# Last stage: residual rows and the experts' second sum through accumulating DMAs, the gates' silu one chunk later

## The chip, the cores and the metric

The kernel runs on one core of a Trainium2 chip. The metric is the device time of one execution in microseconds (us): 5662.19 us, the median of 3 runs (5662.12 to 5663.08). The engines are called by short names: PE is TensorE (PEld its weight loads), DVE is VectorE, ACT is ScalarE, POOL is GpSimd, SP is SyncE, which here only starts transfers.

## What is computed

Four sequences of 2048 tokens with 256 channels go through two layers. The first is a Mamba scan gated by two layers of local attention. The second, to which the change belongs, ends like this in the reference (cut):

```python
xn = _layernorm(x)
s = _L1_attn_ref(xn, ...)        # linear attention over gelu(q)+0.21, gelu(k)+0.21, then
                                 # (res - mu) / sqrt(var + 1e-12) * gamma + beta, res = out + xn
g = _silu(_L1_ffn_ref(xn, ...))  # 64 experts, the best 6 per token, 128 slots each, plus a shared expert
return x + s * g
```

`x` on the last line is the residual: the result of the first layer. The argument of the silu is a sum of three things: the shared expert and the contributions of the routed experts.

## The kernel before, in words

The program runs in blocks, one after the other. In each block every engine has its own written-out list of instructions in order, and semaphores tie them together; no planner is at work. The blocks are set-up, the scan (`mamba`), `layers` (local attention, its gated parts, and `route`), `experts` and `final`.

`route` goes through the 8192 tokens in 16 chunks of 512 (a tile of 128 partitions x 4 x 256). `store_sum` writes the mixed rows x to the DRAM tensor `x1_d`, `store_norm` writes xn and the scores to `xe_d`; the shared expert's output goes to `y_d`, and `odd_d` is cleared.

`experts` goes through the 64 experts. POOL gathers 128 rows per expert with an indirect DMA (L2424) and adds the weighted results back by an indirect accumulating DMA (L2439), even experts into `y_d` (`moe_out`), odd ones into `odd_d` (`moe_odd`). Meanwhile SP loads the first tiles that the last stage needs (`FirstTiles`, `last_stage_chunk`), for chunks 0 and 1 also the residual rows `x1`.

`final` is the last stage, 16 chunks again. Names in the profile are those of the tiles: `ym` is fym, `yo` is fyo, `s1` is fs, `o` is fo, `rot` is frot, `qT` is fqT, `tab` is ftab, `rs` is frs, `x1` is fx. Per chunk c:

- SP (`load_rows`, `load_sums`): loads ym and yo from `y_d` and `odd_d`, xn and x1, three buffers each; a buffer is free when the residual add of the chunk three before it is done (`s_fin`). Then SP waits for `s_fin` of chunk c and stores s1 to the output. ACT's queue loads the transposed xn (`xT`). Each is 512 KB.
- PE: `queries(c+1)` (L2545), then `attend(c)`: L2566 for the normaliser and L2576 for the output. L2566 waits until DVE has read the one buffer p_z of the chunk before (L2676).
- ACT: `queries(c+1)` (L2616, gelu), then `gates(c+1)` (L2622, silu of ym), which waits for POOL's `join`. In the first four chunks `keep_tables` (L2607), which copies the turned rope tables out of PSUM, stands ahead of them in the list.
- DVE: `rotate(c+1)` (L2645), `normaliser(c)` (L2676 zz, L2681 rz, L2714 variance of chunk c-1, L2688 o = p_o * rz, L2694 o += xn), `finish(c-1)` (L2724, L2730, L2735: subtract mean, gamma, rstd, beta, gate), `moments(c)` (L2702, L2708). In three iterations `key_means` is added.
- POOL: `power(c)` (L2760, rstd from the variance, wanted by L2730), `join(c+2)` (L2775, ym += yo; it waits for `s_re`, that is for L2694 of chunk c+1), `residual(c)` (L2767, s1 += x1, after L2735 of chunk c).

Of the kernel before, what the change touches and what calls it, by code (L numbers as in the profile page):

```python
# [8 lines left out]
F32 = mybir.dt.float32  # L9
# [62 lines left out]
def program(nc, A, out, book):  # L72
    xs = nc.dram_tensor("stream", [NS * SLOTS * P, D], F32).ap()
    ssm_out = nc.dram_tensor("ssm_out", [CH + T, D], F32).ap()
    x1_d = nc.dram_tensor("x1", [T, D], F32).ap()
    xe_d = nc.dram_tensor("rows_and_scores", [T, ROW], F32).ap()
# [12 lines left out]
    with ExitStack() as top:  # L89
        def const(name, shape, dt=F32):  # L90
            return top.enter_context(nc.sbuf_tensor(name, shape, dt))

        ident = const("ident", [P, P])
        identb = const("identb", [P, P], BF16)
        mhalf = const("mhalf", [P, 2 * H])
        zrow = const("zrow", [P, D])
        take, put = const("take", [P, NE], I32), const("put", [P, NE], I32)

        with nc.cleanup_on_exit(), ExitStack() as ctx:
            setup(nc, ctx, ident, identb, mhalf, zrow)  # L100
        with nc.cleanup_on_exit(), ExitStack() as ctx:
            mamba(nc, ctx, A, rows, x_in, ssm_out, qk_d, ident, mhalf, zrow)

        cs = const("rope", [P, CPB, CT, 2, D])
        with nc.cleanup_on_exit(), ExitStack() as ctx:
            layers(nc, ctx, A, rows, x_in, ssm_out, x1_d, xe_d, xt_d, y_d, odd_d, kv_d, qk_d, take, put, ident, identb, mhalf,
                   zrow, cs)
        with nc.cleanup_on_exit(), ExitStack() as both:
            first = FirstTiles(nc, both)
            with nc.cleanup_on_exit(), ExitStack() as ctx:  # L110
                experts(nc, ctx, A, x1_d, xe_d, xt_d, y_d, odd_d, kv_d, take, put, ident, first)
            with nc.cleanup_on_exit(), ExitStack() as ctx:
                final(nc, ctx, A, x1_d, xe_d, xt_d, y_d, odd_d, kv_d, out_rows, ident, mhalf, first, cs)

# [1530 lines left out]

def layers(nc, ctx, A, rows, x_in, ssm_out, x1_d, xe_d, xt_d, y_d, odd_d, kv_d, qk_d, take, put, ident, identb, mhalf, zrow, cs):


    bottom = nc.sbuf_base
    with ExitStack() as own:  # L1650
# [6 lines left out]
        g1 = gated(nc, ctx, A, rows, 1, ident, mhalf, gt, at, a1)  # L1657
    rt = route(nc, ctx, A, rows, x_in, ssm_out, x1_d, xe_d, xt_d, y_d, odd_d, kv_d, take, put, ident, mhalf, zrow, cs,
               gt.top - bottom, high - gt.top, g1)
# [51 lines left out]

def route(nc, ctx, A, rows, x_in, ssm_out, x1_d, xe_d, xt_d, y_d, odd_d, kv_d, take, put, ident, mhalf, zrow, cs, first_gap, second_gap, before):

# [79 lines left out]
    def sync(sp):  # L1793
# [651 lines left out]

def final(nc, ctx, A, x1_d, xe_d, xt_d, y_d, odd_d, kv_d, out_rows, ident, mhalf, first, cs):
# [4 lines left out]
    xn, x1 = (t + [sb(f"{n}{k}", [P, CT, D]) for k in range(2, NB)] for t, n in ((first.xn, "fxn"), (first.x1, "fx1")))
    ym, yo = ([sb(f"{n}{k}", [P, CT, D]) for k in range(NB)] for n in ("fym", "fyo"))
    xT, kv, w_q, brow, blk, gam, bet = first.xT, first.kv, first.w_q, first.brow, first.blk, first.gam, first.bet
# [34 lines left out]
    with nc.Block() as block:  # L2488
        @block.sync
        def _(sp):  # L2490
            def load_sums(f):
                k = f % NB
                if f >= NB:
                    sp.wait_ge(s_fin, f - NB + 1)
                sp.dma_start(ym[k][:], tiles(y_d[f * CH + 1:(f + 1) * CH + 1, :])).then_inc(s_ym[k], 16)
                sp.dma_start(yo[k][:], tiles(odd_d[f * CH + 1:(f + 1) * CH + 1, :])).then_inc(s_yo[k], 16)

            def load_rows(f):
                k, rowsf = f % NB, slice(f * CH, (f + 1) * CH)
# [99 lines left out]
        def _(act):  # L2599
# [28 lines left out]
            queries(0)  # L2628
            gates(0)
            for c in range(NC):  # L2630
                if c + 1 < CPB:
                    keep_tables(c + 1)
                if c + 1 < NC:
                    queries(c + 1)
                    gates(c + 1)

        @block.vector
        def _(dve):
# [77 lines left out]
            def finish(c):  # L2716
                k = c % 2
                if c > 1:
                    dve.wait_ge(s_out[k], 16 * (c // 2))
                if c == 0:  # L2720
                    dve.wait_ge(s_gb, 32)
                dve.wait_ge(s_mv, c + 1)
                for j in range(CT):
                    ins = dve.scalar_tensor_tensor(out=s1[k][:, j], in0=o[k][:, j], scalar=mv[k][:, j, 0:1],  # L2724
                                                   in1=gam[:], op0=ALU.subtract, op1=ALU.mult)
# [9 lines left out]
                dve.tensor_tensor(out=s1[k][:], in0=s1[k][:], in1=ym[c % NB][:], op=ALU.mult).then_inc(s_gate, 1)  # L2735

# [20 lines left out]
        def _(pool):  # L2757
# [79 lines left out]
```

## Time and profile before

| | |
|---|---|
| median of 3 runs | 5662.19 us |
| the profiled execution, its own time | 5660.84 us |
| its span in the profile | 5659.1 us |
| busy over the span | PE 87%, PEld 52%, DVE 75%, ACT 52%, POOL 52% |
| last stage (from the first instruction of `final` at 5393.8 us) | 265 us of the span |
| one chunk in the middle of the last stage | 14.79 us |
| HBM read and written | 425.05 MB and 180.37 MB |

The profile is one execution on the chip. Times of rows are in us from the start of the span. "Busy" of an engine is the time in which it executes instructions; a row of the timeline or of the groups names the line, the engine, the operation, the tile written and the tiles read, and in brackets how long the engine sat idle before it and which instruction released it. The share of an engine over the whole span says little about a stage: the last stage is 5% of the span and has its own limit.

### The profile page before, as it was taken

How to read it: one execution, taken by the hardware profiler on the slowest of the kernel's cores; microseconds unless marked ns; L12 is line 12 of the kernel's file. 1: busy time of each engine (PE TensorE's matmuls, PEld its weight loads, DVE VectorE, ACT ScalarE, POOL GpSimd, SP SyncE). 2: the span in 40 equal slices, each digit the busy share in tenths (PEclk: the TensorE clock that was granted, in tenths of full speed). 3: DMA queues.
4: the chain of work that ended last, by engine and by line, in shares of the span. 5: the costliest groups of instructions: out<-in, count | busy, mean ns of one | idle time of the engine just before them, and what ended most of it. 6: DMA issues, size and time to landing. Idle time of an engine off the chain costs nothing. (4 is left out here: it accounts for less than half of the span.)

```text
span 5659.1 us, 79616 instructions
## 1 busy us (share of the span) xinstructions
PE 4948.7 (87%) x26068; PEld 2924.1 (52%) x26068; DVE 4225.2 (75%) x8753; ACT 2969.3 (52%) x6267; POOL 2968.3 (52%) x1603
## 2 busy tenths in 40 slices
PE   7788778777876599999999999999999999998876
PEld 2223223222322377777555566666665556666765
DVE  3999999999999799999433377777763338994279
ACT  4776776776776477777211255555541114452232
POOL 4999889988998556556111244444421010004733
PEclk9898999988987699999999999999999999999987
DMA  5665566556555222323112111111111134445645
GB/s 132 146 156 143 131 150 152 147 131 148 149 146 123 69 90 83 91 91 108 44 49 73 44 35 35 38 35 37 53 42 56 56 104 157 154 143 143 174 159 180
DMA packets 501470, 593.79 MB, mean 105 GB/s; under 512 B 59702, under 2 KB 380996, under 8 KB 496964
## 3 DMA queue, kind: packets, MB, share of 16 engines
q1 hardware_dynamic: 486756, 579.36, 37.3%
q10 hardware_dynamic: 2016, 7.34, 0.4%
q0 software_dynamic: 12288, 2.00, 0.3%
q8 instruction: 211, 3.46, 0.3%
q14 instruction: 199, 1.63, 0.1%
HBM read 425.05 MB, written 180.37 MB: 107 GB/s over the span
## 5 line engine op out<-in xcount | busy, mean ns | idle before, releaser
L654 POOL TENSOR_TENSOR db<-durep,brep 128x2048 f32<-128x2048 f32 x256 | 1161.8, 4538 | 187.9 <-DVE p_h L561 176.9
L513 ACT ACTIVATE p_h<-dlrep,am 128x512 f32<-128x512 f32 x1024 | 704.4, 691 | 195.7 <-DVE hh L572 170.7
L561 DVE TENSOR_TENSOR_SCAN p_h<-p_h,hlast,db 128x512 f32<-128x512 f32 x576 | 716.4, 1273 | 0.0
L349 PE MATMUL p_acc<-hh,fold 128*32 128x512 f32 x2048 | 315.5, 692 | 341.9 <-DVE hh L572 340.7
L1267 POOL TENSOR_TENSOR rot_cos<-rot_cos,rot_sin 128x1024 f32<-128x1024 f32 x128 | 302.5, 2363 | 535.4 <-DVE rot_sin L1188 535.4
L1263 POOL TENSOR_TENSOR rn<-n,mhalf 128x16 f32<-128x16 f32 x128 | 375.2, 2931 | 265.7 <-DVE n L1198 265.6
L572 DVE TENSOR_TENSOR hh<-p_h,crep 128x512 f32<-128x512 f32 x768 | 513.0, 668 | 0.0
L1630 POOL TENSOR_TENSOR grstd<-grstd,mhalf 128x4 f32<-128x4 f32 x32 | 32.6, 1019 | 730.7 <-DVE grstd L1547 730.5
L945 PE MATMUL p_s<-qkT 64*128 64x128 f32 x4096 | 300.0, 286 | 75.7 <-DVE nb L1153 74.6
L1532 ACT ACTIVATE gg<-p_s,b 128x512 f32<-128x512 f32 x160 | 110.0, 687 | 449.0 <-PE p_o L1475 266.2
L1056 ACT ACTIVATE probB<-probB,nb 128x256 f32<-128x256 f32 x512 | 254.3, 499 | 164.7 <-DVE nb L1153 164.7
L642 POOL TENSOR_TENSOR hh<-hs,crep 128x512 f32<-128x512 f32 x256 | 328.2, 1282 | 12.8 <-DVE hs L561 12.8
L349 PEld LDWEIGHTS p_acc<-hh,fold 128*32 128x32 f32 x2048 | 42.4, 114 | 559.9 <-DVE hh L572 535.4
L945 PEld LDWEIGHTS p_s<-qkT 64*128 64x128 f32 x4096 | 250.6, 189 | 129.0 <-DVE nb L1153 105.6
L1475 PE MATMUL p_s<-ghT,w 128*128 128x512 f32 x640 | 302.9, 596 | 5.2 <-DVE ghid L1584 3.6
L1496 PE MATMUL p_t<-w,ghid 128*128 128x256 f32 x1280 | 284.8, 382 | 0.0
L976 PE MATMUL p_o<-probT,v 128*64 128x128 f32 x4096 | 280.2, 279 | 3.0 <-DVE probT L1171 3.0
L561 DVE TENSOR_TENSOR_SCAN hs<-p_h,hlast,db 128x512 f32<-128x512 f32 x192 | 244.0, 1271 | 49.2 <-ACT p_h L513 46.8
L1067 ACT ACTIVATE probT<-p_t 128x512 f32<-128x512 f32 x256 | 152.1, 594 | 232.5 <-PE p_t L962 232.5
L1171 DVE COPY probT<-p_t 128x512 f32<-128x512 f32 x256 | 175.9, 687 | 127.9 <-PE p_t L962 127.8
L502 ACT ACTIVATE hlast<-p_h 128x1 f32<-128x1 f32 x576 | 95.4, 166 | 329.8 <-DVE hh L572 328.7
L227 PE MATMUL p_f<-mxT,w_in 128*128 128x512 f32 x512 | 260.1, 655 | 8.1 <-ACT mxT L390 5.5
(285 smaller groups left out, 11939.4 us busy)
## 6 DMA issues: line engine op xcount, KB each, us to landing
dlrep<-delta_rows SPq DMA_DIRECT2D x256, 256.0 KB
durep<-drive_rows SPq DMA_DIRECT2D x256, 256.0 KB
ew<-in_L_ffn_w SPq DMA_DIRECT2D x192, 176.0 KB
first_queries_keys<-qs SPq DMA_DIRECT2D x128, 256.0 KB, 2.1
qk<-first_queries_keys SPq DMA_DIRECT2D x64, 512.0 KB, 3.8
brep<-bc_rows SPq DMA_DIRECT2D x64, 256.0 KB
crep<-bc_rows SPq DMA_DIRECT2D x64, 256.0 KB
delta_rows<-dl SPq DMA_DIRECT2D x64, 256.0 KB
```

The source lines that it names most:

```text
L349: ins = pe.matmul(p_acc[32 * j:32 * j + 32, :], fold[:], hh[s % 2][:, j], start=False, stop=(g == NG - 1), skip_group_check=True)
L513: act.activation(p_h[:, (i % BANKS) * CH:(i % BANKS + 1) * CH], dlrep[use % 2][:, j], ACT.Exp, scale=am[:, q, j, g:g + 1]).then_inc(s_ex, 1)
L561: dve.tensor_tensor_scan(out=state, data0=bank, data1=db[s % 2][:, j], initial=0.0 if first else hlast[:, i % TILES:i % TILES + 1], op0=AL ...
L572: dve.tensor_tensor(out=hh[s % 2][:, j], in0=p_h[:, (i % BANKS) * CH:(i % BANKS + 1) * CH], in1=crep[c % 2][:, s % NG], op=ALU.mult).then_ ...
L642: pool.tensor_tensor(out=hh[s % 2][:, 0], in0=hs[s % 2][:], in1=crep[c % 2][:, s % NG], op=ALU.mult).then_inc(s_hp, 1)
L654: pool.tensor_tensor(out=db[s % 2][:], in0=durep[use % 2][:], in1=brep[c % 2][:, g:g + 1, :].to_broadcast([P, 4, CH]), op=ALU.mult).then_i ...
L945: ins = pe.matmul(p_s[:, at:at + P], here[g * DK:(g + 1) * DK, c:c + P], there[g * DK:(g + 1) * DK, INNER + c:INNER + c + P], start=True, ...
L976: ins = pe.matmul(p_o[g * DK:(g + 1) * DK, (h // 2) * P:(h // 2 + 1) * P], vv[u][:, h * DK:(h + 1) * DK], probT[:, j, w, :], start=(w == 0 ...
L1263: pool.tensor_tensor(out=rn[f % 2][:], in0=n2[f % 2][:], in1=mhalf[:], op=ALU.pow).then_inc(s_rn, 1)
L1267: pool.tensor_tensor(out=rc[:], in0=rc[:], in1=rsn[:], op=ALU.add).then_inc(s_rot, 1)
L1475: ins = pe.matmul(dst[:], w1[:, f, o + j * P:o + (j + 1) * P], hT[:, f, :], start=(f == 0), stop=(f == DH - 1))
L1496: ins = pe.matmul(p_y[:, j0 * D:(j0 + 1) * D], hid[:, j, j0 * P:(j0 + 1) * P], w2[:, j, :], start=False, stop=(j == FB - 1), skip_group_ch ...
```

## The change

Six edits, all in or for the last stage:

1. The residual rows are stored by `route` straight into the output tensor instead of `x1_d`, which is gone. The loads of x1 (two in `experts`, fourteen in `final`) are gone with their tiles and semaphores.
2. POOL's `residual(c)` no longer adds: it issues a DMA that adds s1 onto the output rows in DRAM (`accum_op`). SP's store of the output and its wait are gone.
3. POOL's `join(c)` no longer adds: after ym has landed it issues a DMA that adds the rows of `odd_d` onto ym in SBUF. The loads of yo and their tiles are gone, and so is the wait for `s_re`.
4. ACT's `gates(c)` waits for that DMA and stands in iteration c, behind `queries(c+1)`, instead of one iteration earlier; `gates(0)` no longer stands ahead of the loop.
5. SP's loads wait for `s_gate` (L2735 done) instead of `s_fin`.
6. s1 has three buffers instead of two; `finish(c)` waits for the accumulating DMA of chunk c-3.

```diff
 # route
-            sp.dma_start(tiles(x1_d[f * CH:(f + 1) * CH, :]), x[f % 2][:]).then_inc(s_sx1[f % 2], 16)
+            sp.dma_start(tiles(out_rows[f * CH:(f + 1) * CH, :]), x[f % 2][:]).then_inc(s_sx1[f % 2], 16)
 # experts, last_stage_chunk
-                sp.dma_start(first.x1[f][:], tiles(x1_d[rowsf, :])).then_inc(first.s_x1[f], 16)
 # final, sync
                 if f >= NB:
-                    sp.wait_ge(s_fin, f - NB + 1)
+                    sp.wait_ge(s_gate, f - NB + 1)
                 sp.dma_start(ym[k][:], tiles(y_d[f * CH + 1:(f + 1) * CH + 1, :])).then_inc(s_ym[k], 16)
-                sp.dma_start(yo[k][:], tiles(odd_d[f * CH + 1:(f + 1) * CH + 1, :])).then_inc(s_yo[k], 16)
...
                 sp.dma_start(xn[k][:], tiles(xe_d[rowsf, 0:D])).then_inc(s_xn[k], 16)
-                sp.dma_start(x1[k][:], tiles(x1_d[rowsf, :])).then_inc(s_x1[k], 16)
...
-                sp.wait_ge(s_fin, c + 1)
-                sp.dma_start(tiles(out_rows[c * CH:(c + 1) * CH, :]), s1[c % 2][:]).then_inc(s_out[c % 2], 16)
 # final, scalar
             def gates(c):
-                act.wait_ge(s_ya, c + 1)
+                act.wait_ge(s_yo[c % NB], 16 * (c // NB + 1))
                 act.activation(ym[c % NB][:], ym[c % NB][:], ACT.Silu).then_inc(s_sy, 1)
...
             queries(0)
-            gates(0)
             for c in range(NC):
                 if c + 1 < CPB:
                     keep_tables(c + 1)
                 if c + 1 < NC:
                     queries(c + 1)
-                    gates(c + 1)
+                gates(c)
 # final, vector, finish(c): s1[k] becomes s1[n], n = c % NB
-                if c > 1:
-                    dve.wait_ge(s_out[k], 16 * (c // 2))
+                if c >= NB:
+                    dve.wait_ge(s_out[n], 16 * (c // NB))
 # final, gpsimd
             def residual(c):
-                pool.wait_ge(s_x1[c % NB], 16 * (c // NB + 1))
                 pool.wait_ge(s_gate, c + 1)
-                pool.tensor_tensor(out=s1[c % 2][:], in0=s1[c % 2][:], in1=x1[c % NB][:], op=ALU.add).then_inc(s_fin, 1)
+                pool.dma_start(tiles(out_rows[c * CH:(c + 1) * CH, :]), s1[c % NB][:],
+                               accum_op=ALU.add).then_inc(s_out[c % NB], 16)
 
             def join(c):
                 k = c % NB
-                if c > 1:
-                    pool.wait_ge(s_re, c)
                 pool.wait_ge(s_ym[k], 16 * (c // NB + 1))
-                pool.wait_ge(s_yo[k], 16 * (c // NB + 1))
-                pool.tensor_tensor(out=ym[k][:], in0=ym[k][:], in1=yo[k][:], op=ALU.add).then_inc(s_ya, 1)
+                pool.dma_start(ym[k][:], tiles(odd_d[c * CH + 1:(c + 1) * CH + 1, :]),
+                               accum_op=ALU.add).then_inc(s_yo[k], 16)
...
+            for k in range(NB):
+                pool.wait_ge(s_out[k], 16 * len(range(k, NC, NB)))
```

## Rows read from the trace of the kernel before

**Rows 1.** Busy time by stretch: one chunk (14.79 us), and the stretch with the lowest clock

```profile
core 0: us, PE busy (x) PEld busy (x) DVE busy (x) ACT busy (x) POOL busy (x), PEclk, DMA share, GB/s
5522.94:5537.73 14.79, 12.27 (x65) 9.99 (x65) 14.41 (x24) 4.89 (x5) 5.89 (x3) 0.84 0.65 206
5565.00:5580.00 15.00, 13.38 (x56) 11.15 (x56) 14.58 (x30) 4.89 (x5) 5.89 (x3) 0.66 0.63 205
```

**Rows 2.** Timeline of PE in the last stage: what its normaliser waits for

```profile
5521.01 3.55 PE L2566 MATMUL fp_z<-fkm,fqT 128*128 128x8 f32 x16 [2.50 <-DVE zz L2676]
```

**Rows 3.** Timeline of DVE, part of one chunk (start, us, engine, line, tiles)

```profile
5521.61 1.23 DVE L2688 TENSOR_TENSOR fo<-fp_o,rz 128x1024 f32<-128x1024 f32 x1
5522.94 1.23 DVE L2694 TENSOR_TENSOR fo<-fo,fxn 128x1024 f32<-128x1024 f32 x1
5524.08 3.77 DVE L2724 SCALAR_TENSOR_TENSOR fs<-fo,fmv,gam 128x256 f32<-128x256 f32 x4
...
5532.47 3.06 DVE L2645 SCALAR_TENSOR_TENSOR frot<-fqT,ftab 128x1024 f32<-128x1024 f32 x2
```

**Rows 4.** Timeline of POOL in the same chunk

```profile
5521.62 1.02 POOL L2760 TENSOR_TENSOR frs<-frs,mhalf 128x4 f32<-128x4 f32 x1 [3.11 <-DVE frs L2714]
5524.25 2.53 POOL L2775 TENSOR_TENSOR fym<-fym,fyo 128x1024 f32<-128x1024 f32 x1 [1.60 <-DVE fo L2694]
5530.97 2.34 POOL L2767 TENSOR_TENSOR fs<-fs,fx 128x1024 f32<-128x1024 f32 x1 [4.19 <-DVE fs L2735]
```

**Rows 5.** Timeline of DVE where POOL is idle beside it

```profile
5410.83 2.36 DVE L2645 SCALAR_TENSOR_TENSOR frot<-fqT,ftab 128x1024 f32<-128x1024 f32 x2 [3.05 <-ACT fqT L2616]
...
5640.47 1.67 DVE L2724 SCALAR_TENSOR_TENSOR fs<-fo,fmv,gam 128x256 f32<-128x256 f32 x4
```

**Rows 6.** The chain that ended last, in order of time, at the stage's start

```profile
5428.71 2.52 POOL fym L2775
5431.26 1.06 ACT fym L2622
...
5433.92 6.22 PE fp_q L2545 x8
```

**Rows 7.** Timeline of PE, ACT and DVE at the stage's start

```profile
5403.74 1.06 ACT L2622 ACTIVATE fym<-fym 128x1024 f32<-128x1024 f32 x1
...
5406.40 3.67 PE L2545 MATMUL fp_q<-fxT,w_q 128*128 128x512 f32 x8 [2.39 <-ACT ftab L2607]
...
5440.98 2.36 DVE L2645 SCALAR_TENSOR_TENSOR frot<-fqT,ftab 128x1024 f32<-128x1024 f32 x2 [3.98 <-ACT fqT L2616]
...
5446.29 1.23 DVE L2688 TENSOR_TENSOR fo<-fp_o,rz 128x1024 f32<-128x1024 f32 x1 [1.10 <-PE fp_o L2576]
```

**Rows 8.** Groups of POOL's instructions in `experts`: gathers and accumulating scatters of 128 rows

```profile
L2424 POOL DMA_INDIRECT ex<-rows_and_scores,take x64 | 67.3, 1051 | 20.2 <-issue 17.1 <-POOL ex L2428 0.9 <-DMA moe_out<-eyb,put 0.9
L2439 POOL DMA_INDIRECT moe_out<-eyb,put x32 | 50.8, 1589 | 29.3 <-DVE eyb L2415 16.5 <-issue 8.3 <-DMA moe_out<-eyb,put 4.5
```

**Rows 9.** DMA queues (packets, MB, share of 16 engines), stretch 5385.5 to 5387.3

```profile
q0 software_dynamic: 117, 0.11, 56.4%
```

**Rows 10.** The same, stretch 5653 to 5660: the last store of the output

```profile
q1 hardware_dynamic: 528, 0.52, 21.1%
```

**Rows 11.** The chain again: a load of yo from its issue to its landing

```profile
5623.54 5.60 DMA fyo<-moe_odd
```

**Rows 12.** Timeline of DVE and POOL at the end of the stage

```profile
5638.00 1.22 DVE L2688 TENSOR_TENSOR fo<-fp_o,rz 128x1024 f32<-128x1024 f32 x1
...
5649.22 1.67 DVE L2730 SCALAR_TENSOR_TENSOR fs<-fs,frs,bet 128x256 f32<-128x256 f32 x4
...
5645.24 2.34 POOL L2767 TENSOR_TENSOR fs<-fs,fx 128x1024 f32<-128x1024 f32 x1 [6.22 <-DVE fs L2735]
5647.69 1.19 POOL L2760 TENSOR_TENSOR frs<-frs,mhalf 128x4 f32<-128x4 f32 x1
5652.30 2.34 POOL L2767 TENSOR_TENSOR fs<-fs,fx 128x1024 f32<-128x1024 f32 x1 [3.42 <-DVE fs L2735]
```

More of the change, by code:

```diff
@@ L105, in program @@
         with nc.cleanup_on_exit(), ExitStack() as ctx:
-            layers(nc, ctx, A, rows, x_in, ssm_out, x1_d, xe_d, xt_d, y_d, odd_d, kv_d, qk_d, take, put, ident, identb, mhalf,
+            layers(nc, ctx, A, rows, x_in, ssm_out, out_rows, xe_d, xt_d, y_d, odd_d, kv_d, qk_d, take, put, ident, identb, mhalf,
                    zrow, cs)
@@ L110, in program @@
             with nc.cleanup_on_exit(), ExitStack() as ctx:
-                experts(nc, ctx, A, x1_d, xe_d, xt_d, y_d, odd_d, kv_d, take, put, ident, first)
+                experts(nc, ctx, A, xe_d, xt_d, y_d, odd_d, kv_d, take, put, ident, first)
             with nc.cleanup_on_exit(), ExitStack() as ctx:
-                final(nc, ctx, A, x1_d, xe_d, xt_d, y_d, odd_d, kv_d, out_rows, ident, mhalf, first, cs)
+                final(nc, ctx, A, xe_d, xt_d, y_d, odd_d, kv_d, out_rows, ident, mhalf, first, cs)
 def allocators(nc, ctx, tag=""):
@@ L1643, in gated, with layers @@
     return Programs(tensor, scalar, vector, gpsimd, sync, s_out, s_y=s_y)
-def layers(nc, ctx, A, rows, x_in, ssm_out, x1_d, xe_d, xt_d, y_d, odd_d, kv_d, qk_d, take, put, ident, identb, mhalf, zrow, cs):
+def layers(nc, ctx, A, rows, x_in, ssm_out, out_rows, xe_d, xt_d, y_d, odd_d, kv_d, qk_d, take, put, ident, identb, mhalf, zrow, cs):
     bottom = nc.sbuf_base
@@ L1657, in layers @@
         g1 = gated(nc, ctx, A, rows, 1, ident, mhalf, gt, at, a1)
-    rt = route(nc, ctx, A, rows, x_in, ssm_out, x1_d, xe_d, xt_d, y_d, odd_d, kv_d, take, put, ident, mhalf, zrow, cs,
+    rt = route(nc, ctx, A, rows, x_in, ssm_out, out_rows, xe_d, xt_d, y_d, odd_d, kv_d, take, put, ident, mhalf, zrow, cs,
                gt.top - bottom, high - gt.top, g1)
@@ L1709, in __init__, with route @@
         self.tensor, self.scalar, self.vector, self.gpsimd, self.sync = tensor, scalar, vector, gpsimd, sync
-def route(nc, ctx, A, rows, x_in, ssm_out, x1_d, xe_d, xt_d, y_d, odd_d, kv_d, take, put, ident, mhalf, zrow, cs, first_gap, second_gap, before):
+def route(nc, ctx, A, rows, x_in, ssm_out, out_rows, xe_d, xt_d, y_d, odd_d, kv_d, take, put, ident, mhalf, zrow, cs, first_gap, second_gap, before):
     sb, ps, sem = allocators(nc, ctx)
@@ L2297, in __init__ @@
         self.kv = [sb(f"fkv{k}", [P, 2 * D]) for k in range(2)]
-        self.xn, self.x1 = ([sb(f"{n}{k}", [P, CT, D]) for k in range(2)] for n in ("fxn", "fx1"))
+        self.xn = [sb(f"fxn{k}", [P, CT, D]) for k in range(2)]
         self.w_q, self.brow, self.blk = sb("w_q", [P, DH, D]), sb("fbrow", [P, D]), sb("fblk", [P, P])
@@ L2301, in __init__, with experts @@
         self.s_w, self.s_blk, self.s_gb = sem("f_weights"), sem("f_blk"), sem("f_gamma_beta")
-        self.s_xT, self.s_kv, self.s_xn, self.s_x1 = (
-            [sem(f"f_{n}{k}") for k in range(2)] for n in ("xT", "kv", "xn", "x1"))
-def experts(nc, ctx, A, x1_d, xe_d, xt_d, y_d, odd_d, kv_d, take, put, ident, first):
+        self.s_xT, self.s_kv, self.s_xn = (
+            [sem(f"f_{n}{k}") for k in range(2)] for n in ("xT", "kv", "xn"))
+def experts(nc, ctx, A, xe_d, xt_d, y_d, odd_d, kv_d, take, put, ident, first):
     sb, ps, sem = allocators(nc, ctx)
@@ L2443, in _, with final @@
                 pool.wait_ge(s_add[e % U], 16 * (NE // U))
[L2446 removed]
+def final(nc, ctx, A, xe_d, xt_d, y_d, odd_d, kv_d, out_rows, ident, mhalf, first, cs):
     sb, ps, sem = allocators(nc, ctx)
     NB, HH = 3, HA // DH
[L2451 to L2452 removed]
+    xn = first.xn + [sb(f"fxn{k}", [P, CT, D]) for k in range(2, NB)]
+    ym = [sb(f"fym{k}", [P, CT, D]) for k in range(NB)]
     xT, kv, w_q, brow, blk, gam, bet = first.xT, first.kv, first.w_q, first.brow, first.blk, first.gam, first.bet
@@ L2461, in final @@
     zz, rz = sb("zz", [P, CT, HA]), sb("rz", [P, CT, HA])
-    o, s1 = ([sb(f"{n}{k}", [P, CT, D]) for k in range(2)] for n in ("fo", "fs1"))
+    o = [sb(f"fo{k}", [P, CT, D]) for k in range(2)]
+    s1 = [sb(f"fs1{k}", [P, CT, D]) for k in range(NB)]
     st = sb("fst", [P, CT, 6])
@@ L2468, in final @@
     s_w, s_blk, s_gb, s_kv, s_xT = first.s_w, first.s_blk, first.s_gb, first.s_kv, first.s_xT
-    s_xn, s_x1 = (t + [sem(f"f_{n}{k}") for k in range(2, NB)] for t, n in ((first.s_xn, "xn"), (first.s_x1, "x1")))
-    s_ym, s_yo = ([sem(f"f_{n}{k}") for k in range(NB)] for n in ("ym", "yo"))
-    s_out = [sem(f"f_out{k}") for k in range(2)]
+    s_xn = first.s_xn + [sem(f"f_xn{k}") for k in range(2, NB)]
+    s_ym, s_yo, s_out = ([sem(f"f_{n}{k}") for k in range(NB)] for n in ("ym", "yo", "out"))
     s_swap, s_bias, s_bq, s_kmt, s_km, s_ksum, s_cst = (
         sem("f_" + n) for n in ("swap", "bias", "bq", "kmt", "km", "ksum", "cst"))
-    s_fill, s_empty, s_z, s_o, s_sy, s_ya = (sem("f_" + n) for n in ("fill", "empty", "z", "o", "sy", "ya"))
-    s_rot, s_zz, s_rz, s_os, s_re, s_st, s_mv, s_va, s_rs, s_ga, s_be, s_gate, s_fin = (
-        sem("f_" + n) for n in ("rot", "zz", "rz", "os", "re", "st", "mv", "va", "rs", "ga", "be", "gate", "fin"))
+    s_fill, s_empty, s_z, s_o, s_sy = (sem("f_" + n) for n in ("fill", "empty", "z", "o", "sy"))
+    s_rot, s_zz, s_rz, s_os, s_re, s_st, s_mv, s_va, s_rs, s_ga, s_be, s_gate = (
+        sem("f_" + n) for n in ("rot", "zz", "rz", "os", "re", "st", "mv", "va", "rs", "ga", "be", "gate"))
     def tables_at(u):
```

11 lines of the change are left out of this document (4 added, 7 removed).

## The prediction

> **What bounds the kernel now.** The page's table by engine says PE 87%, which is a mean over stages and decides nothing here: the change touches the last 265 us (and one store target in `route`, two loads in `experts`). So I read the last stage by stretches first. In one chunk of 14.79 us DVE is busy 14.41, PE 12.27, POOL 5.89, ACT 4.89, and the DMA engines 0.65 of the time [rows 1]. The timeline of PE gives the direction: its normaliser L2566 sat idle 2.50 us until DVE had read p_z (L2676) [rows 2], so PE's waits follow DVE and not the reverse. The chain of waits agrees: from 5446 us to the end it is a list of DVE lines with almost nothing else. DVE bounds the stage, and what the change is worth is what it takes off DVE.
>
> On the face of it that is nothing, since both removed adds run on POOL. The timelines of the two engines side by side say otherwise. DVE's L2724 (four small instructions) takes 3.77 us in the chunk, and POOL's join L2775 starts 0.17 us after it and lasts 2.53 [rows 3, 4]; at the end of the stage, with no join beside it, the same four take 1.67 [rows 5]. The two L2645 take 3.06 us where POOL's residual add L2767 (5530.97 to 5533.31) reaches into them, and 2.36 with POOL idle [rows 3 to 5]. So DVE loses 3.77 - 1.67 = 2.10 and 3.06 - 2.36 = 0.70 us per chunk. What does not suffer: L2688, which runs beside POOL's power L2760 and still takes 1.23 [rows 3, 4].
>
> The Trainium skill ("SBUF — State Buffer", Who interferes with whom) has a rule for this: a VectorE instruction with two SBUF inputs and a GpSimd instruction that reads SBUF exclude each other for whole instructions, and the one that comes second waits. The trace agrees: L2724 and L2645 read two SBUF tensors and wait, 2.10 us for a 2.53 us join; L2688 reads one from PSUM and does not. The same section says that writing DMA descriptors wants the write side of that port, which such a VectorE instruction doesn't take; by that, the new DMAs would cost DVE nothing.
>
> **The change part by part.** Durations are from the profiled execution (5660.84 us, 1.35 below the median of the runs); the sum is made against it.
>
> *Joins and residual adds off POOL.* The chunks' L2688 start from 5446.29 (chunk 2) to 5638.00 (chunk 15) [rows 7, 12], 13 intervals. Each holds one join (chunks 3 to 15): 13 x 2.10 = 27.3 us. The residual adds of chunks 1 to 12 reach into a rotate (after chunk 12 there is none left to rotate): 12 x 0.70 = 8.4 us. Together 35.7 us, all on DVE, hence on the path. The new period is 14.79 - 2.80 = 11.99 us.
>
> *ACT's list at the start.* Before, the chain runs through POOL's join of chunk 2 (which waits for L2694 of chunk 1), ACT's silu behind it, the tables L2607 queued behind the silu, and PE's queries, 6.22 us of them [rows 6]. DVE then idles 3.98 us for ACT's gelu, 1.10 us for PE, and loses one join's 2.10 in that interval [rows 3, 5, 7]. After, no join waits for `s_re` and the silu stands behind tables and queries: 3.98 + 1.10 + 2.10 = 7.2 us go. Earlier still, silu(0) (1.06 us and a table load before it) stands on ACT ahead of tables(1), and PE waits 2.39 for them [rows 7]: about 2.1 us. Sum 9.3, I take 9. What the moved silu now waits for is an accumulating DMA; behind it on ACT are tables and queries of the next iteration. For chunks 0 and 1 it should land before 5411 us, and silu(0) now comes up at about 5410, so there is little room: if it lands some 5 us late, 5 of the 9 are lost. Range 4 to 9.5.
>
> *Issuing the two DMAs on POOL.* No row shows a direct DMA on POOL. A gather of 128 rows holds POOL 1.05 us, an accumulating scatter of 128 rows 1.59 [rows 8]. A DMA here has 512 rows. If the price is per instruction it is 1.6 us (1.05 at least), if per row 4 x 1.59 = 6.4. I take the middle, 4.0. POOL then needs per chunk 2 x 4.0 + 1.02 (power) + 3 gaps of 0.3 = 9.9 us of 11.99: hidden. In order: residual(c-1) is issued from L2735's end on, which lies 4.9 us before the next variance (5530.97 to 5521.62 + 14.79, less the 0.70 [rows 1, 4]) and 9 us before L2730 wants power(c), so it hides up to about 5.3 us each (2D + 1.9 <= 12). Behind power(c) is join(c+2): ym was loaded after L2735 of chunk c-1, by a load that takes 5.6 us [rows 11], about when power ends. Behind that join waits residual(c), which has until the buffer's next use, 3 chunks later. Silu(c+2) is wanted more than a chunk after its join: hidden.
>
> *DMA engines.* Before: six 512 KB transfers a chunk (ym, yo, xn, x1, xT, out), 0.65 x 14.79 = 9.6 us, 1.6 each [rows 1]. After: three plain ones, 4.8, and two accumulating ones. The last full scatter-add moved 117 packets in 0.564 x 1.8 = 1.02 us of 16 engines, 8.7 ns a packet; a plain store 528 in 0.211 x 7 = 1.48, 2.8 ns [rows 9, 10]. So between 1.5 and 4.6 us per accumulating transfer. The small one is thin (a few rows per engine, latency showing), so I take 3.2, twice a plain one, as it reads two operands: 4.8 + 6.4 = 11.2 of 11.99. It fits, without much to spare; three buffers each hide the lateness. For the landing the skill ("DMA: Bandwidth & Descriptors", Anatomy of one DMA) gives about 2.0 us + bytes / 436 GB/s, 3.2 us for 512 KB; here a plain load took 5.6, and no row shows the accumulating kind.
>
> *SP, buffers, loads.* SP's list gets shorter and its loads start some 2.5 us earlier (no POOL add in between); they were not on the path. The third s1 buffer only moves a wait three chunks back: 0. `route` stores the same bytes elsewhere: 0. In `experts` two loads of 512 KB go, 3 us of DMA at 0.8 load where PE sets the pace: 0, at most 2 us gained.
>
> *The tail.* The last two chunks have no joins; DVE's work is as before. Power(15) stands behind residual(14): now L2735(14)'s end + 0.15, issue 4.0, power 1.19 and 0.44 for the hand-overs = 5.8, against the 4.1 us after which L2730 starts now (L2735(14) ends 0.15 before 5645.24; L2730 starts at 5649.22 [rows 12]): 1.7 us later. After L2735(15), which ends 0.15 before 5652.30, the span goes on for 6.95 us (add, store, landing). Then: 0.15 + 4.0 issue + 0.5 until packets move + 2.8 to 3.2 for them + 1.9 from the last packet to the end = 9.5: 2.5 us more. With an issue of 1.05 and a plain-like transfer the tail is 2 shorter, with 6.4 and 4.6 about 10 longer.
>
> Sum: 35.7 + 9 - 4.2 = 40.5 us off 5660.8, 5620.3; beside the median that is 5621.7, say **5622 us**.
>
> **The rivals.**
> 1. *POOL's DMA instruction holds DVE's second input like an add does* (the slower side). For it: in this stage both kinds of POOL instruction that run beside two-SBUF-input DVE instructions make them wait [rows 3, 4]; in `experts`, where POOL issues DMAs, DVE has no such instruction, so nothing contradicts. Against: a DMA issue reads no tile. With 4.0 us each, the join would cost DVE 4.0, the residual 4.0 less the 1.8 of statistics that stand first: 6.2 against 2.8 now, 3.4 x 13 = 44 us lost, 9 won at the start, 4 lost in the tail: 5701. It decides for slower from an issue of about 2.5 us on.
> 2. *The DMA engines become the bound*: at 4.6 us per accumulating transfer, 4.8 + 9.2 = 14.0 a chunk; 2.0 x 13 = 26 of the gain go, and 1.5 in the tail: 5650.
> 3. *POOL's issue becomes the bound*: at 6.4, 12.8 + 1.9 = 14.7 a chunk; 2.7 x 13 = 35 go and 5 more in the tail: 5662, no change.
> 4. *PE becomes the bound.* It needs 12.27 us a chunk at a granted clock of 0.84 and 13.38 at 0.66 [rows 1]. For it: that is above 11.99. Against: the clock fell behind PE's own waits for DVE; with those gone it should stay nearer 1.0, and in the middle of the stage DVE's L2688 shows no wait for PE's output [rows 3]. At 13.4: 1.4 x 13 = 18 go, 5640.
>
> **How the numbers follow.** Forecast as told 0.58 (own range 5613 to 5632, from start and tail); rival 1 0.10; rival 2, in full or in part, 0.13; rival 3, mostly in part, 0.09; rival 4 0.10. Under 0.2% (11 us) this kernel's measurement can't tell from no change. Faster by more: the forecast, rival 4, most of 2 and a third of 3: 0.80. Same: the rest of 2 and part of 3, 0.08. Slower: rival 1 and the worst of 2 and 3 together, 0.12. The range 5610 to 5655 leaves out rival 1 and the far ends of 2 and 3.
>
> **What would show it.** Right: L2724 x4 at 1.7 us and L2645 x2 at 2.4 in every chunk, L2688 to L2688 in 12.0 us, DMA share near 0.9, POOL DMA issues between 1.6 and 5 us, the end 8 to 10 us after the last L2735. Wrong: L2724 or L2645 still stretched beside POOL's DMA lines (rival 1); DVE idle for xn or `s_out`, or ACT's gelu late behind a silu that waits for the accumulate (2); L2730 late behind L2760 (3); L2688 late behind L2576 with the clock low (4).

## The result

The kernel after takes **5618.12 us** (median of 4 runs, 5616.72 to 5619.14) against 5662.15 before (4 runs, 5661.75 to 5663.08): ratio 0.9922, 95% interval 0.991 to 0.9933. That is 44 us off, where 40.5 were forecast. The spans of the two profiled executions differ by 42.5 us (5659.1 and 5616.6), and the readings below account for that. Executions of one program differ by up to 6 us (5657.77 to 5663.52 for the kernel before in a series of 21).

### The profile page after: what moved, and what is told of

Same layout as the page of the kernel before. It is cut to its first block and busy times, and to the rows that moved or that the text cites. A ratio compares the mean times of both kernels' runs of the same rounds, so it can differ in the third digit from the quotient of the medians.

```text
span 5616.6 us, 79533 instructions
## 1 busy us (share of the span) xinstructions
PE 4923.3 (88%) x26068; PEld 2902.3 (52%) x26068; DVE 4185.3 (75%) x8753; ACT 2967.1 (53%) x6265; POOL 2931.7 (52%) x1603
## 3 DMA queue, kind: packets, MB, share of 16 engines
q1 hardware_dynamic: 461412, 554.19, 36.4%
```

## The profile after

First the groups of the last stage, stretch 5375 to 5620 (line, engine, operation, count, busy us, mean ns of one, idle us before them and what ended it). L2715 was L2724 before, L2636 was L2645, L2763 the join, L2757 the residual row.

```profile
L2636 DVE SCALAR_TENSOR_TENSOR frot<-fqT,ftab 128x1024 f32<-128x1024 f32 x32 | 37.3, 1208 | 4.9 <-ACT fqT L2608 4.9
L2715 DVE SCALAR_TENSOR_TENSOR fs<-fo,fmv,gam 128x256 f32<-128x256 f32 x64 | 26.7, 479 | 0.0
L2763 POOL DMA_DIRECT2D fym<-moe_odd x16 | 21.0, 1310 | 10.7 <-DMA fym<-moe_out 10.5
L2757 POOL DMA_DIRECT2D out<-fs x16 | 20.5, 1281 | 82.9 <-DVE fs L2726 79.0 <-DMA out<-fs 3.9
```

No instruction of either DVE group is stretched any more, and a direct DMA holds POOL 1.3 us. Next one chunk on DVE's timeline, which answers to [rows 3] (start, us, engine, line).

```profile
5510.91 1.22 DVE L2679 TENSOR_TENSOR fo<-fp_o,rz 128x1024 f32<-128x1024 f32 x1
5512.24 1.23 DVE L2685 TENSOR_TENSOR fo<-fo,fxn 128x1024 f32<-128x1024 f32 x1
5513.38 1.67 DVE L2715 SCALAR_TENSOR_TENSOR fs<-fo,fmv,gam 128x256 f32<-128x256 f32 x4
5515.08 1.67 DVE L2721 SCALAR_TENSOR_TENSOR fs<-fs,frs,bet 128x256 f32<-128x256 f32 x4
5516.79 1.22 DVE L2726 TENSOR_TENSOR fs<-fs,fym 128x1024 f32<-128x1024 f32 x1
...
5519.66 2.33 DVE L2636 SCALAR_TENSOR_TENSOR frot<-fqT,ftab 128x1024 f32<-128x1024 f32 x2
...
5522.87 1.22 DVE L2679 TENSOR_TENSOR fo<-fp_o,rz 128x1024 f32<-128x1024 f32 x1
```

POOL beside it, for [rows 4]:

```profile
5510.93 1.03 POOL L2751 TENSOR_TENSOR frs<-frs,mhalf 128x4 f32<-128x4 f32 x1 [3.13 <-DVE frs L2705]
5511.93 1.30 POOL L2763 DMA_DIRECT2D fym<-moe_odd  x1
5518.31 1.27 POOL L2757 DMA_DIRECT2D out<-fs  x1 [5.08 <-DVE fs L2726]
```

L2679 to L2679 is 11.96 us, with no idle gap; it was 14.79 [rows 1]. The join's issue lies beside L2685, two SBUF inputs, which still takes 1.23. By stretches of 12 us, for [rows 1]:

```profile
core 0: us, PE busy (x) PEld busy (x) DVE busy (x) ACT busy (x) POOL busy (x), PEclk, DMA share, GB/s
5500.00:5512.00 12.00, 9.19 (x58) 6.96 (x57) 11.62 (x25) 5.81 (x6) 3.62 (x5) 0.99 0.93 230
5512.00:5524.00 12.00, 12.00 (x57) 9.99 (x57) 11.62 (x25) 4.04 (x5) 3.61 (x4) 0.73 1.09 231
```

DVE is the bound at 11.62 of 12.00 in both. In the first stretch PE is busy 9.19 us at a granted clock of 0.99, the upper of its two levels (1.2 and 2.4 GHz); in the second it is busy all 12.00 us at a mean of 0.73, between them. The DMA share is above 1 in the second, of which more below. The start of the stage, for [rows 7]:

```profile
5403.65 2.12 ACT L2599 ACTIVATE ftab<-fp_q 128x512 f32<-128x512 f32 x4 [0.19 <-PE fp_q L2526]
...
5411.14 1.06 ACT L2614 ACTIVATE fym<-fym 128x1024 f32<-128x1024 f32 x1
```

The tables no longer stand behind silu(0), and silu(0) finds its sum landed. Chunk 2, in which DVE idled 3.98 for ACT and 1.10 for PE [rows 7], now has no idle time in it:

```profile
5433.86 2.33 DVE L2636 SCALAR_TENSOR_TENSOR frot<-fqT,ftab 128x1024 f32<-128x1024 f32 x2
...
5438.11 1.22 DVE L2679 TENSOR_TENSOR fo<-fp_o,rz 128x1024 f32<-128x1024 f32 x1
```

The end, for [rows 12], POOL first, then DVE, then the DMA queue from 5609 to the end:

```profile
5602.89 1.20 POOL L2751 TENSOR_TENSOR frs<-frs,mhalf 128x4 f32<-128x4 f32 x1 [0.40 <-DVE frs L2705]
5607.99 1.31 POOL L2757 DMA_DIRECT2D out<-fs  x1 [3.90 <-DMA out<-fs]
```

```profile
5604.42 1.67 DVE L2721 SCALAR_TENSOR_TENSOR fs<-fs,frs,bet 128x256 f32<-128x256 f32 x4
5606.12 1.22 DVE L2726 TENSOR_TENSOR fs<-fs,fym 128x1024 f32<-128x1024 f32 x1
```

```profile
q0 software_dynamic: 528, 0.52, 54.3%
```

The last accumulating store takes 0.543 x 7.6 = 4.13 us of 16 engines; the plain one took 1.48 [rows 10]. Over the whole stage the 32 accumulating DMAs of both kinds take 3.5 us each (49.6% of 225.6 us). From L2726's end (5607.34) to the end of the span it is 9.26 us, 6.95 before.

One small DVE instruction near the end is shorter too: the one for the last variance, 0.75 us before, beside POOL's residual add (5645.24 to 5647.58, [rows 12]), and 0.17 after, with no add there:

```profile
5646.86 0.75 DVE L2714 TENSOR_SCALAR frs<-fmv 128x4 f32<-128x4 f32 x1
```

```profile
5602.63 0.17 DVE L2705 TENSOR_SCALAR frs<-fmv 128x4 f32<-128x4 f32 x1
```

It reads one tile only, so two SBUF inputs are not the only case in which DVE waits for a POOL add. Experiments 1 and 2, which keep that add, show 0.74 in the same place; no experiment was made for it.

**The account.** Start of the stage to L2679 of chunk 2: 52.46 before, 43.13 after, -9.33. The 13 intervals to chunk 15: 191.71 and 155.65 (5438.11 to 5593.76), -36.06. Tail: 21.10 and 22.84, +1.74. The stage itself started 1.15 later, which is no part of the change: over the profiled executions of all kernels here its first gelu starts anywhere from 5397.6 to 5402.5. Sum -42.5, the difference of the spans.

## The experiments

Each kernel is the one before or the one after with one thing changed (the eleventh with two). Ratios are to the kernel before, timed beside it: 5662.14 us for experiments 1, 2, 3 and 9, 5662.37 for 4 to 7, and 5657.27 for 8, 10 and 11. The kernel after was not timed again, so differences to its 5618.12 can be off by as much as the kernel before moved, some 5 us in the last group; there the stage itself is compared in the profiled executions.

**1. The order alone.** The kernel before, with the silu moved:

```
-            gates(0)
             for c in range(NC):
...
                     queries(c + 1)
-                    gates(c + 1)
+                gates(c)
```

> The kernel before with one edit: ACT's gates(c) stands in iteration c behind queries(c+1), gates(0) no longer ahead of the loop; joins and residual adds stay on POOL. Theory (POOL's adds hold DVE's second input; the order on ACT is worth only the start): tables no longer wait behind a silu, PE's 2.39 us wait and DVE's 3.98 + 1.10 us go, every L2724 group stays at 3.8 us and L2645 at 3.06. 5662 - 7 = 5655 us. Rival (the order and the dropped waits are the whole gain, the adds cost DVE nothing that matters): about 5620 us.

5654.17 against 5662.14, ratio 0.9987 (0.9978 to 0.9996): 8.0 us. DVE's stalls stay, as a chunk of its timeline shows. So the order by itself gives only the start: in the profiled execution the stage up to chunk 2's o = p_o * rz is 6.48 us shorter than before (45.98 against 52.46), the 13 intervals are the same (191.76 against 191.71).

```profile
5509.98 3.06 DVE L2644 SCALAR_TENSOR_TENSOR frot<-fqT,ftab 128x1024 f32<-128x1024 f32 x2
```

**2. The join's DMA with the order**, residual add left on POOL:

```
-                pool.tensor_tensor(out=ym[k][:], in0=ym[k][:], in1=yo[k][:], op=ALU.add).then_inc(s_ya, 1)
+                pool.dma_start(ym[k][:], tiles(odd_d[c * CH + 1:(c + 1) * CH + 1, :]),
+                               accum_op=ALU.add).then_inc(s_yo[k], 16)
```

> The kernel before with the joins as accumulating DMAs and the silu one chunk later; residual add on POOL and store by SP as before. Theory: the 2.10 us of each join go (13 in the steady part, one at the start) and the start's 7 us: 5662 - 27 - 2 - 7 = 5626 us; L2724 x4 at 1.67 us, L2645 x2 still at 3.06 us. Rival (DMA engines near their limit take it back): above 5635 us.

5625.70, ratio 0.9938 (0.9925 to 0.9952): 36.4 us. The groups of stretch 5375 to 5655 show which half of the stall is gone and which stays (1507 ns for a rotate, 1208 in the kernel after):

```profile
L2643 DVE SCALAR_TENSOR_TENSOR frot<-fqT,ftab 128x1024 f32<-128x1024 f32 x32 | 47.0, 1507 | 4.9 <-ACT fqT L2615 4.9
L2722 DVE SCALAR_TENSOR_TENSOR fs<-fo,fmv,gam 128x256 f32<-128x256 f32 x64 | 26.7, 478 | 0.0
```

**3. The residual's DMA alone**, join add, its wait and the early silu put back:

```
-                pool.dma_start(ym[k][:], tiles(odd_d[c * CH + 1:(c + 1) * CH + 1, :]),
-                               accum_op=ALU.add).then_inc(s_yo[k], 16)
+                pool.tensor_tensor(out=ym[k][:], in0=ym[k][:], in1=yo[k][:], op=ALU.add).then_inc(s_ya, 1)
```

> The kernel after with the join back on POOL (loads of yo, wait for s_re) and the silu back in its early place; only the residual goes by accumulating DMA. Theory: 12 x 0.70 = 8.4 us go in the rotates, the tail is about 2 us longer: 5656 us; L2724 x4 stays at 3.8 us. Rival: the accumulate onto the output is what pays (fewer loads, SP's queue free): under 5640 us.

5653.87, ratio 0.9988 (0.9979 to 0.9997): 8.3 us, with the other half of the stall:

```profile
L2717 DVE SCALAR_TENSOR_TENSOR fs<-fo,fmv,gam 128x256 f32<-128x256 f32 x64 | 56.0, 934 | 0.0
L2638 DVE SCALAR_TENSOR_TENSOR frot<-fqT,ftab 128x1024 f32<-128x1024 f32 x32 | 37.4, 1209 | 8.9 <-ACT fqT L2609 8.9
```

Experiments 2 and 3 add to 44.7 us; the whole change gave 44.0. In the 13 intervals the profiled executions give 27.16 us for the joins (164.55 left) and 8.85 for the residual adds (182.86 left), together 36.01 of the 36.06.

**4. A read put back on POOL.** The kernel after, with an add of two constant 128x1024 tiles in 14 chunks, where the join add was; its result is not used:

```
                     join(c + 2)
+                    pool.wait_ge(s_re, c + 2)
...
+                    pool.tensor_tensor(out=xtr[:, 0:CT * D]..., in0=cs[:, 0, :, 0, :], in1=cs[:, 1, :, 0, :], op=ALU.add)...
```

> The kernel after with one more POOL instruction per chunk in the place where the join's add stood (behind L2694 of the next chunk, by the same wait): an add of two constant tiles of 128 x 1024 into a scratch tile, 14 times; its result isn't used. Theory (a POOL instruction that reads SBUF and a DVE instruction with two SBUF inputs exclude each other): the L2715 group (L2724 before) goes back from 1.67 to about 3.8 us in 14 chunks, 14 x 2.1 = 29 us: 5647 us. Rival (the stretch before came from the data flow around the join or from the loads of yo, not from POOL reading): 5618 us, L2715 at 1.67.

5647.66 (nine of ten runs; the tenth took 13942 us), ratio to the kernel before 0.9975 (0.9965 to 0.9985): 29.5 us more than the kernel after, 2.11 for each of the 14 adds. The two engines' timelines:

```profile
5499.38 3.77 DVE L2716 SCALAR_TENSOR_TENSOR fs<-fo,fmv,gam 128x256 f32<-128x256 f32 x4
```

```profile
5499.55 2.53 POOL L2776 TENSOR_TENSOR fxtr<-rope 128x1024 f32<-128x1024 f32 x1 [0.33 <-DVE fo L2686]
```

**5. A fill of the same length in the same place**, which reads no SBUF:

```
+                    pool.memset(xtr[:], 0.0).then_inc(s_xtr, 1)
```

> The same place, but the POOL instruction is a fill of 2900 columns with zero, about 2.5 us long, that reads nothing. Theory (only POOL's reads collide): L2715 stays at 1.67 us, 5618 us. Rival (any POOL instruction on SBUF holds DVE): 5647 us as with the add.

5618.54 (5616.84 to 5619.15), ratio to before 0.9924: nothing.

```profile
5499.79 1.67 DVE L2716 SCALAR_TENSOR_TENSOR fs<-fo,fmv,gam 128x256 f32<-128x256 f32 x4
```

```profile
5499.94 2.51 POOL L2776 MEMSET fxtr<- 128x2900 f32 x1 [0.29 <-DVE fo L2686]
```

So it is not POOL being busy, and not its writes: for the join's add it is its reads of SBUF beside an instruction of DVE with two SBUF inputs. "SBUF — State Buffer", Who interferes with whom, in the Trainium skill makes that distinction (against an instruction that only writes, such a DVE instruction does not contend), and these two runs agree: 2.11 us and 0. For the residual add no such pair was run; that its 0.70 us in the rotate go with it is what experiments 1 to 3 show.

**6. A plain store in place of the accumulating one**; this kernel leaves the residual sum out of the output:

```
-                pool.dma_start(tiles(out_rows[...]), s1[c % NB][:], accum_op=ALU.add).then_inc(s_out[c % NB], 16)
+                pool.dma_start(tiles(out_rows[...]), s1[c % NB][:]).then_inc(s_out[c % NB], 16)
```

> The kernel after, but POOL's DMA of the output is a plain store without accumulation (the residual is left out of the output). The transfer should take about 1.5 us of all engines instead of 4.1, POOL's instruction about as long as now if its price is per instruction. Theory (DVE bounds the steady part, the accumulate costs only in the tail): the steady period stays at 11.96 us, the end comes 2.5 to 4 us sooner, 5615 us. Rival (the accumulating traffic costs the steady part too): under 5610 us.

5614.35 (5612.82 to 5617.03), 3.8 us below the kernel after. One issue costs POOL 0.80 us in place of 1.28. In the profiled execution the 13 intervals are the same 155.65 us, and the tail behind them is 2.73 us shorter (20.11 against 22.84): the accumulate in DRAM costs its 2 to 3 us once, at the end. Of these, 0.52 are the shorter last issue and 2.2 the packets, which run for 1.8 us here and for 4.0 in the kernel after.

```profile
L2757 POOL DMA_DIRECT2D out<-fs x16 | 12.9, 804 | 82.4 <-DVE fs L2726 82.4
```

**7 and 8. More load on the DMA engines**: in each of 14 chunks one, and two, more loads of 512 KB into tiles nobody reads:

```
+                for i in range(1):
+                    sp.dma_start(junk[k][i][:], tiles(y_d[rowsf, :])).then_inc(s_junk[k], 16)
```

> The kernel after with one more plain load of 512 KB per chunk (14 in all) into tiles that nobody reads. If the measured DMA shares (about 0.97 of 11.96 us, 11.6 us a chunk) are the capacity that is used, 1.6 us more make it 13.2 us a chunk and the stage is bound by DMA: 13 x 1.2 = 16 us, 5634 us. Rival (packet times overlap and stretch under load, there is room): within 3 us of 5618.

> The kernel after with two more plain loads of 512 KB per chunk (28 in all) into tiles that nobody reads. One more changed nothing (5617.8) although the summed share of packet times passed 1. If there is a real limit near it, it must show now: two loads are 3.2 us of all engines at the rate of a lone transfer, on top of 3 x 1.6 + about 3 + 4 = 11.8: 15 us a chunk, 5650 us or more. Rival (the packet times of the accumulating DMAs are mostly waiting, in which other packets move; real need 5 x 1.6 + 2 x 1.6 = 11.2): within 3 us of 5618, period 11.96.

5617.79 (5616.93 to 5618.99) with one load: equal to the kernel after, so there the theory of the full engines fell and its rival held. With two, 5618.38 (5615.48 to 5619.99), ratio 0.9930 (0.9915 to 0.9945): within 3 us of 5618 as the rival says, but only 38.9 us below the kernel before timed beside it. The 13 intervals of the stage tell the two apart, first the kernel after, then one load, then two:

```profile
5438.11:5593.76 155.65, 131.48 (x726) 105.92 (x724) 150.29 (x320) 59.74 (x61) 46.59 (x39) 0.87 0.96 207
5438.42:5594.07 155.65, 131.37 (x726) 105.81 (x724) 150.29 (x320) 59.71 (x61) 46.57 (x39) 0.87 1.07 251
5433.98:5595.29 161.31, 133.12 (x726) 107.59 (x724) 150.73 (x320) 58.68 (x60) 47.30 (x39) 0.85 1.14 282
```

One load is free: the same 155.65 us, while the DMA share goes from 0.96 to 1.07 and the traffic from 207 to 251 GB/s. Two cost 5.66 us in all, 0.44 a chunk, where the theory of the full engines had 32; this execution hides it, since its stage happened to begin 3.7 us earlier (at 5391.26 against 5394.98). What is late is the sum: POOL's joins wait 64.9 us in all for ym to land (10.5 in the kernel after), the silu comes late behind them, the next gelu behind the silu, and DVE's idle time before the rotates, all for that gelu, is 10.2 us instead of 4.9. The added loads stand on SP's queue with those of ym, so a busy queue and busy engines are not separated here.

The share adds up the time in which packets are under way. That most of an accumulating packet's time is waiting, in which others pass, would fit these rows; it was not measured by itself. A share near 1 did not mean full engines.

**9. Another tail.** The kernel after, but in the last chunk SP has the residual rows loaded ahead into a tile of their own, DVE multiplies and adds in two halves, and SP stores each half plainly:

```
+                    for h in range(2):
+                        hs = slice(2 * h, 2 * h + 2)
+                        dve.tensor_tensor(out=s1[n][:, hs], in0=s1[n][:, hs], in1=ym[c % NB][:, hs], op=ALU.mult)...
+                        dve.tensor_tensor(out=s1[n][:, hs], in0=s1[n][:, hs], in1=xl[:, hs], op=ALU.add).then_inc(s_half, 1)
```

> The kernel after, but the last chunk does without the accumulating DMA: SP loads its residual rows ahead of time into a tile of its own, DVE multiplies by the gate and adds them in two halves, and SP stores each half. Theory (the end after the last gate is 9.26 us because the accumulating transfer takes 4.1 us of all engines and lands late; the plain store was 1.5): the end comes about 4 us sooner, 5614 us. Rival (the end is fixed by the accumulate of chunk 14 still under way): within 1 us of 5618.

5614.16 (5613.25 to 5614.61), 4.0 us below. In its timeline the last add starts at 5607.00 and the span ends at 5611.4, 3.7 us after that add is done; the 13 intervals are the same 155.65 us, and the tail is 4.03 us shorter (18.81):

```profile
5607.00 0.69 DVE L2741 TENSOR_TENSOR fs<-fs,fxl 128x512 f32<-128x512 f32 x1
```

**10. The silu back in its early place**, both DMAs kept:

```
+            gates(0)
             for c in range(NC):
...
-                gates(c)
+                    gates(c + 1)
```

> The kernel after with ACT's silu back in its early place (gates(c+1) in iteration c, gates(0) ahead of the loop). Theory (the new place matters only at the start, where tables and queries would wait behind a silu that waits for an accumulating DMA): the start loses 8 to 10 us, the steady period stays 11.96: 5627 us. Rival (three buffers hide it, the place is worth nothing): 5618 us.

5655.23 against 5657.27 for the kernel before beside it (5653.77 to 5660.33 there), ratio 0.9997 (0.9988 to 1.0006): the whole gain is gone. I had expected 5627. One chunk of it, ACT first, then DVE:

```profile
5516.95 1.06 ACT L2614 ACTIVATE fym<-fym 128x1024 f32<-128x1024 f32 x1 [10.10 <-DMA fym<-moe_odd]
...
5518.03 1.28 ACT L2608 ACT_TABLE_LOAD   x1
5519.32 1.27 ACT L2608 ACTIVATE fqT<-fp_q,b_q 128x512 f32<-128x512 f32 x2
```

```profile
5509.94 1.22 DVE L2680 TENSOR_TENSOR fo<-fp_o,rz 128x1024 f32<-128x1024 f32 x1
...
5520.70 2.36 DVE L2637 SCALAR_TENSOR_TENSOR frot<-fqT,ftab 128x1024 f32<-128x1024 f32 x2 [1.93 <-ACT fqT L2608]
...
5523.94 1.23 DVE L2680 TENSOR_TENSOR fo<-fp_o,rz 128x1024 f32<-128x1024 f32 x1
```

This chunk takes 14.00 us, and here are no stretched instructions: it is a closed loop. DVE's variance releases POOL's power, behind which the join is issued (5510.95 to 5512.25), whose sum lands 4.7 us later; the silu waits for it, the gelu of the next queries stands behind the silu, and DVE's rotate waits 1.93 us for that gelu. Against the kernel after, the start of the stage is 15.75 us longer (58.88 against 43.13 to chunk 2), where 8 to 10 were expected, and the 13 intervals 25.0 (180.65 against 155.65), where none were. In the kernel after, the gelu stands ahead of the silu and is done over 9 us before its rotate (5519.66); the waits for the DMA are still there, but what is behind them, a gate of DVE's and the next gelu, has some 8 us to spare:

```profile
5508.91 1.27 ACT L2608 ACTIVATE fqT<-fp_q,b_q 128x512 f32<-128x512 f32 x2
5510.19 1.28 ACT L2614 ACT_TABLE_LOAD   x1
5519.36 1.06 ACT L2614 ACTIVATE fym<-fym 128x1024 f32<-128x1024 f32 x1 [7.89 <-DMA fym<-moe_odd]
```

**11. A faster version.** Experiment 9, and ACT (under half busy) does the subtraction and the scale in four instructions a chunk, the bias -mean x rstd coming from a small instruction each on DVE and POOL. DVE keeps gamma and beta as two instructions over the whole tile, in place of the eight small ones of L2715 and L2721, and takes the chunk's statistics ahead of them:

```
+                for j in range(CT):
+                    ins = act.activation(s1[n][:, j], o[k][:, j], ACT.Identity, bias=nb[k][:, j], scale=rs[k][:, j])
...
+                dve.tensor_tensor(out=s1[n][:], in0=s1[n][:], in1=gam[:].unsqueeze(1).to_broadcast([P, CT, D]),
+                                  op=ALU.mult).then_inc(s_ga, 1)
```

> The kernel with the new tail and less work on DVE: ACT computes (o - mean) * rstd (Identity with bias and scale per partition, 4 per chunk, bias by one small DVE and one small POOL instruction), DVE then needs two whole-tile instructions (gamma, beta) of about 1.14 us start to start instead of the two groups of 1.70; moments stand ahead of finish. Theory (DVE alone bounds the steady part, DMA and PE have room): the period falls by 0.8 to 1.0 us to about 11.1, 13 of them, less some 2 us at the end: 5605 us. Rival (PE at its mixed clock, or the DMA engines, hold the period at 11.9): 5615 us or more.

**5605.32** (5603.86 to 5608.79), ratio to before 0.9909 (0.9894 to 0.9924), where the kernel before had 5657.27 beside it: 52 us below, where the kernel after was 44 below its own. So it is some 8 us faster than the kernel after, not the 13 between the two medians; in the profiled executions the stage takes 213.68 us against 221.62, 7.94 less. A chunk takes 11.19 us (5504.21 to 5515.40), as expected, and the two whole-tile instructions 2.42 in place of 3.34. The 13 intervals are 10.09 us shorter (145.56), but the tail is 22.77 us where experiment 9 alone had 18.81: in the last chunk DVE sits idle 5.02 us for ACT's subtraction and scale. That the median met the expected 5605 owes something to luck, since this execution's stage began 4.3 us earlier than that of the kernel after.

```profile
5508.54 1.19 DVE L2738 TENSOR_TENSOR fs<-fs,gam 128x1024 f32<-128x1024 f32 x1
5509.77 1.23 DVE L2741 TENSOR_TENSOR fs<-fs,bet 128x1024 f32<-128x1024 f32 x1
```

## Why the prediction was right, and where not

- *DVE bounds the stage, and POOL's adds cost it 2.10 and 0.70 us a chunk: right.* 35.7 us were forecast for the 13 intervals, 36.06 measured; both instruction groups run at their unstretched length, and experiments 2 and 3 split the sum into 27.16 (27.3 forecast) and 8.85 (8.4). That the add's reads cost it was argued from two groups of rows; experiments 4 and 5 show it for the join (2.11 us, and 0).
- *The start, worked out as 9.3, taken as 9: right* at 9.33. The doubt about a late silu(0) was not needed. The parts came as forecast too: 2.12 before chunk 0 (2.1), 7.20 between chunks 1 and 2 (7.2). The order alone gives 6.48 of the 9.33 (experiment 1).
- *"Silu(c+2) is wanted more than a chunk after its join: hidden": right only for the place that the change gives it*, and the prediction credited the move with the start alone. Experiment 10 puts 15.75 us on it at the start and 25.0 in steady state: the DMA's latency stands in a list of ACT, and whether the gelu is behind it or ahead decides over the whole gain. The prediction named what is queued behind the new wait, "tables and queries of the next iteration", but not what a place one step earlier would do.
- *The issue on POOL, taken as 4.0 between 1.05 and 6.4: three times too high.* It measured 1.28 to 1.33. The price goes by the instruction, not by the row: 512 rows cost less than the 1.59 of an accumulating scatter of 128 [rows 8]. Rival 3 is out.
- *DMA time per accumulating transfer, taken as 3.2: too low into DRAM*, 4.13 at the last store, inside the bounds; over both kinds it was 3.5. The sum of 11.2 us a chunk was near (a share of 0.96 is 11.5 us). *"It fits, without much to spare": wrong as reasoned.* Summed packet time was read as capacity used; one more load a chunk, with the share at 1.07, changes nothing, and two cost 5.66 us in all (experiments 7 and 8). Rival 2 did not come; that it would not have at 4.6 us either is argued from experiment 8, whose two loads add as much packet time (2 x 1.48 us a chunk) and cost a fifth of its 26 us.
- *The tail, +4.2: measured +1.74; the term that was mis-sized.* The 1.7 us for power(15) behind an issue of 4.0 did not come, since the issue is short. Instead DVE's part became 0.57 shorter (14.15 to 13.58), because L2714 no longer waits for the residual add (0.75 and 0.17), which the prediction had at nothing ("DVE's work is as before"). The 2.5 for issue and landing came as 2.31, and that is luck: the issue was taken 2.7 too long, and the wait before it, the packets and the end too short by 0.5, 1.0 and 0.9 (0.65 until the issue, 1.31 for it, 0.5 until packets move, 4.0 for them, 2.8 behind the last). The 1.9 us of the forecast come from a last store that SP issued; experiment 6, whose last store is plain but issued by POOL, has 2.8 as well, so the difference goes with the store being POOL's and not with the accumulate. "DMA: Bandwidth & Descriptors", Anatomy of one DMA, in the Trainium skill gives by estimate 3.2 us for 512 KB from POOL, most of the fixed 2.0 us being the write's receipt; here 7.3 us passed from the issue's end to the end of the span, and 5.1 with a plain store (experiment 6). A long receipt fits, the size does not.
- *Rival 1 (the DMA instruction holds DVE's second input): out.* L2685 took 1.23 beside the join's issue, and no L2715 or L2636 is longer than with POOL idle.
- *Rival 4 (PE becomes the bound): out.* The clock alternates between 0.99 and 0.73 by stretches and PE fills the slow ones, but DVE's L2679 waited 2.9 us for PE in the whole stage.

The sum was 3.5 us short of the 44.0 between the medians: 2.5 from the tail, 0.7 from joins and start, -1.15 from the later start of the stage; the remaining 1.5 lie between the profiled executions and the medians.

**Open:** why POOL's last issue started 0.65 us after DVE's last instruction, where 0.3 is usual in the stage. The row names an earlier store's landing, but experiment 6 shows the same 0.65 with plain stores and with DVE named, so that is not it. Why the span goes on for 2.8 us behind the last packet of a store of POOL's and 1.9 behind one of SP's was not tested.

## What to carry to other kernels

An engine that looks idle enough to take an elementwise pass may be charging the bound engine for it: compare the same instruction's duration with and without the neighbour beside it, and price the neighbour by that difference, whatever its own busy time. If a DMA does the pass instead, its latency goes into whoever reads the result; move that reader behind the work of its engine that the bound engine waits for, and take the last piece, which nothing hides, off the slow path by hand. Test a resource that looks full by adding load before a plan is built on it.

## What the runs showed of the hardware

- A direct DMA of 512 rows of 1 KB holds POOL 1.28 to 1.33 us when it accumulates and 0.80 when it doesn't, and DVE at 11.62 of 12.00 us busy did not hold up its issue.
- An accumulating store of 512 KB into DRAM has 4.13 us of packet time over 16 engines, a plain one 1.48. The span ended 2.8 us after the last packet of a store that POOL issued, accumulating (kernel after) or plain (experiment 6), and 1.9 us after that of a plain one from SP (kernel before, experiment 9). The accumulating load into SBUF was used by ACT 4.7 us after its issue ended in experiment 10, and 6.1 in the chunk shown of the kernel after.
- A POOL add of 2.53 us costs a DVE instruction group with two SBUF inputs 2.1 us; a POOL fill of 2.51 us costs it nothing. A DVE instruction with one input (TENSOR_SCALAR, L2714) took 0.75 us beside a POOL add and 0.17 without.
- The profile's DMA share can exceed 1. Over the 13 intervals it was 0.96, 1.07 and 1.14 with none, one and two more loads a chunk, at 207, 251 and 282 GB/s; the first load cost nothing, the second 5.7 us in all.
